# Row halves of TensorE for two heads in both attention stages of a two-layer transformer kernel

## What is computed

```python
x = x + attn_a(layernorm(x));  x = x + ffn(layernorm(x))
x = x + attn_b(layernorm(x));  x = x + ffn(layernorm(x))

# attn_a: 16 heads of 16, causal, T = 2048
att = softmax(where(causal, q @ k.T / sqrt(16), -inf))
att = att * decay_weight_matrix(T)      # zero from a lag of 511 on; the softmax sum still takes all keys
y = (att @ v) @ W_proj
# attn_b: 16 heads of 16, causal, with biases, no decay
y = layernorm(softmax(...) @ v @ Wo + bo) * gamma + beta
# ffn: gelu(x @ binarize(w1).T + b1) @ binarize(w2).T + b2
```

## Time and profile before

| | us |
|---|---|
| median of 3 runs | 2740.55 (2735.39 to 2742.51) |
| the profiled execution | 2736.11 |
| its span | 2734.4 |
| TensorE busy in the span | 2454.8 (90%) |
| VectorE busy | 1958.3 (72%) |
| ScalarE busy | 1515.6 (55%) |
| GpSimd busy | 1052.5 (38%) |

### The profile page before, as it was taken

The page is one execution under the profiler, slowest core; times in us unless marked ns, Lnnn a source line. Parts: engine busy times, 40 slices in busy tenths (PEclk is TensorE's granted clock), DMA queues, the critical chain, the costliest instruction groups (busy, mean ns, idle before and its releaser), DMA issues. The chain is left out here.

```text
span 2734.4 us, 44488 instructions
## 1 busy us (share of the span) xinstructions
PE 2454.8 (90%) x13984; PEld 1404.0 (51%) x13984; DVE 1958.3 (72%) x4863; ACT 1515.6 (55%) x3309; POOL 1052.5 (38%) x1274
## 2 busy tenths in 40 slices
PE   4959999999999999969997599999999999997788
PEld 2535545454544545437774355555555555553676
DVE  5667787777787777716663588888888888870786
ACT  1218576776767685734332056666666666664333
POOL 0037777777777777751221301000101001011653
PEclk8969999999999999989998589999999999998999
DMA  4994142332505050033544751423505234102110
GB/s 134 252 144 63 24 56 36 44 51 32 70 11 75 13 69 6 5 114 77 125 96 98 111 75 16 64 38 44 70 15 72 32 51 62 18 7 99 47 54 31
DMA packets 181847, 171.03 MB, mean 63 GB/s; under 512 B 90352, under 2 KB 131056, under 8 KB 180848
## 3 DMA queue, kind: packets, MB, share of 16 engines
q1 hardware_dynamic: 181616, 168.18, 35.0%
HBM read 105.98 MB, written 61.08 MB: 61 GB/s over the span
## 5 line engine op out<-in xcount | busy, mean ns | idle before, releaser
L704 POOL TENSOR_TENSOR att_a_wd<-att_a_wt,decay 128x256 f32<-128x256 f32 (+3 forms) x896 | 754.6, 873 | 259.8 <-PE att_a_po L907 122.7
L742 ACT ACTIVATE att_b_wt<-att_b_ps 128x512 f32<-128x512 f32 (+3 forms) x1280 | 589.4, 539 | 354.6 <-PE att_b_ps L882 352.6
L782 DVE TENSOR_REDUCE att_a_mpart<-att_a_pm 128x1 f32<-128x512 f32 x768 | 513.5, 687 | 132.2 <-PE att_a_pm L860 129.0
L782 DVE TENSOR_REDUCE att_b_mpart<-att_b_pm 128x1 f32<-128x512 f32 x768 | 503.7, 686 | 109.7 <-PE att_b_pm L860 107.7
L860 PE MATMUL att_a_pm<-att_a_kop,att_a_qop 128*128 128x512 f32 (+3 forms) x1280 | 522.6, 426 | 55.6 <-DMA att_a_qop<-att_a_qop 28.2
L742 ACT ACTIVATE att_a_wt<-att_a_ps 128x512 f32<-128x512 f32 (+3 forms) x896 | 430.8, 506 | 218.1 <-PE att_a_ps L885 131.6
L860 PE MATMUL att_b_pm<-att_b_kop,att_b_qop 128*128 128x512 f32 (+3 forms) x1280 | 503.0, 408 | 36.6 <-DMA att_b_qop<-att_b_qop 29.9
L882 PE MATMUL att_b_ps<-att_b_qop,att_b_kop 128*128 128x512 f32 (+3 forms) x1280 | 453.2, 383 | 6.6 <-ACT att_b_wt L742 3.4
L722 POOL TENSOR_SCALAR_AFFINE_SELECT att_b_wt<-att_b_wt 128x512 f32<-128x512 f32 x128 | 81.6, 637 | 867.1 <-ACT att_b_wt L742 867.1
L860 PEld LDWEIGHTS att_a_pm<-att_a_kop,att_a_qop 128*128 128x128 f32 x1280 | 240.6, 193 | 324.6 <-DVE att_a_mpart L782 130.2
L860 PEld LDWEIGHTS att_b_pm<-att_b_kop,att_b_qop 128*128 128x128 f32 x1280 | 246.3, 194 | 277.1 <-DVE att_b_mpart L782 112.0
(11 more groups left out here) (174 smaller groups left out, 2622.6 us busy)
## 6 DMA issues: line engine op xcount, KB each, us to landing
att_a_kop<-qk SPq DMA_DIRECT2D x128, 128.0 KB, 7.7
att_a_qop<-qk SPq DMA_DIRECT2D x128, 128.0 KB, 8.0
att_b_kop<-qk SPq DMA_DIRECT2D x128, 128.0 KB, 6.2
att_b_qop<-qk SPq DMA_DIRECT2D x128, 128.0 KB, 6.8
qk<-qkv_a_qk_hi SPq DMA_DIRECT2D x32, 256.0 KB, 4.7
qk<-qkv_a_qk_lo SPq DMA_DIRECT2D x32, 256.0 KB, 4.5
qk<-mid_qk_hi SPq DMA_DIRECT2D x32, 256.0 KB, 4.0
qk<-mid_qk_lo SPq DMA_DIRECT2D x32, 256.0 KB, 4.5
```

Of the source, the lines that this page charges most:

```text
L704: pool.tensor_tensor(wd[:, kq % 2, j, a:z], wt[:, kq % buffers, j, a:z], keep["decay"][:, u:u + z - a], ALU.mult).then_inc(w_decayed, 1)
L742: act.activation(wt[:, kq % buffers, j, a:CH], pe_[:, seen % EBANKS, 0:CH - a], ACT.Exp)\
L782: dve.tensor_reduce(mpart[:, c, piece, u:u + 1], pm[:, n % MBANKS, 0:w], AX.X, ALU.max, negate=True).then_inc(m_reduced, 1)
```

## The change

The 4 heads of a group become 2 pairs. Heads 0 and 1 (index j) lie on partitions 0 to 63 and heads 2 and 3 on partitions 64 to 127 of `kop` and `qop`, which are half as wide as before; there is no padding. Every M and every S of the plan now stands for two heads, a = 0 and a = 1, and issues a matmul on rows 0 to 63 and one on rows 64 to 127, into two banks. The maxima are no longer a row of `qop`: they go to a tile `mx` of their own, at row 0 and row 64, with zeros elsewhere, and each S issues a second pair of matmuls, `ones_row` x `mx`, that adds them. `mx` has one buffer for each chunk, so MC waits for the scores of the group before. The mask of att_a becomes two matmuls of 64 columns for each head. MC takes 8 transfers of half the length, the loads of a chunk take 16 of half the size, and the copy of the zero row is gone. Bank counts, buffers and widths of a unit stay.

```diff
@@ attention_plan
-            follow(number + 1, GH - 1, ("PV", c, kb))
+            follow(number + 1, 1, ("PV", c, kb))
-        for j in range(GH):
-            e.append((60.0 + CH - P * max(0, kb - TB * c), ("S", c, kb, j)))
+        for j in range(GH // 2):
+            e.append((2 * (60.0 + CH - P * max(0, kb - TB * c)), ("S", c, kb, j)))
...
-                    n += 1
+                    n += 2
@@ spaced
-            follow((3, 0.0, ("MC", c)))
+            follow((2, 0.0, ("MC", c)))
             if far(c, decayed):
-                follow((8, 0.0, ("FE", c)), (11, 0.0, ("FM", c)))
+                follow((4, 0.0, ("FE", c)), (6, 0.0, ("FM", c)))
@@ attention, tiles
-        kop = sb("kop", [P, 2, GH, T], F32R)
-        qop = sb("qop", [P, 2, NC, GH, CH], F32R)
+        kop = sb("kop", [P, 2, GH // 2, T], F32R)
+        qop = sb("qop", [P, 2, NC, GH // 2, CH], F32R)
+        mx = sb("mx", [P, NC, GH // 2, CH], F32R)
@@ SP, load
-                for r in range(PAIRS):
...
-                if g < 2:
-                    sp.wait_ge(q_padded[par], c + 1)
-                sp.dma_start(qop[MROW:MROW + 1, par, c, :, :].bitcast(F32),
-                             qop[96:97, par, c, :, :].bitcast(F32)).then_inc(qk_in[par][c], 16)
+                for a in range(2):
+                    heads = slice(head(0, a), head(0, a) + GH // 2)
+                    for r in range(PAIRS):
...
@@ SP, MC
                         sp.wait_ge(mrow_ready, done(g + d, c))
+                        if g + d > 0:
+                            sp.wait_ge(e_scores, scored(g + d - 1, c))
...
+                        for a in range(2):
+                            row = mx[HALF * a:HALF * a + 1, c, :, :].bitcast(F32)
+                            row = row.rearrange("o j (t k i) -> o (j t) k i", t=TB, k=P // SQUARE)
+                            for k in range(P // SQUARE):
+                                unit = SQUARE * k + TB * head(0, a)
+                                sp.dma_start(row[:, :, k, :], mrow[unit:unit + UNITS // 2, c, :].bitcast(F32))\
+                                  .then_inc(m_in[c], 16)
@@ TensorE, M
-                        mm = pe.matmul(pm[:, bank, 0:w], qop[:, mpar, c, j, qb * P:(qb + 1) * P],
-                                       kop[:, mpar, j, piece * CH:piece * CH + w], start=True, stop=True)
-                        mm.then_inc(m_scores, 1)
+                        for a in range(2):
+                            pe.wait_ge(m_reduced, M_UNITS * (g + d) + max(n + a + 1, MBANKS))
+                            if FARS:
+                                pe.wait_ge(f_done, FAR_UNITS * (g + d) + far_left(n + a) + MBANKS)
+                            mm = pe.matmul(pm[:, (n + a) % MBANKS, 0:w], qop[rows(a), mpar, c, j, qb * P:(qb + 1) * P],
+                                           kop[rows(a), mpar, j, piece * CH:piece * CH + w], start=True, stop=True)
+                            mm.then_inc(m_scores, 1)
@@ TensorE, S
-                        mm = pe.matmul(pe_[:, bank, 0:CH - a], kop[:, par, j, kb * P:(kb + 1) * P],
-                                       qop[:, par, c, j, a:CH], start=True, stop=not diagonal)
-                        if diagonal:
-                            mm = pe.matmul(pe_[:, bank, 0:P], keep["identr"][:, :], keep["mask_k"][:, :],
-                                           start=False, stop=True)
-                        mm.then_inc(e_scores, 1)
-                        e += 1
+                        for a in range(2):
+                            pe.wait_ge(e_weights, E_UNITS * g + max(e + a + 1, EBANKS))
+                            pe.matmul(pe_[:, banks[a], 0:CH - z], kop[rows(a), par, j, kb * P:(kb + 1) * P],
+                                      qop[rows(a), par, c, j, z:CH], start=True, stop=False)
+                        for h in range(2 if decayed and kb >= TB * c else 0):
+                            for a in range(2):
+                                pe.matmul(pe_[:, banks[a], HALF * h:HALF * (h + 1)],
+                                          keep["tri"][rows(a), (0, 1, 2, 0)[2 * a + h], :],
+                                          keep["identr"][rows(a), rows(a)], start=False, stop=False)
+                        for a in range(2):
+                            mm = pe.matmul(pe_[:, banks[a], 0:CH - z], keep["ones_row"][rows(a), :],
+                                           mx[rows(a), c, j, z:CH], start=False, stop=True)
+                            mm.then_inc(e_scores, 1)
+                        e += 2
```

144 lines of the change are left out of this document (69 added, 75 removed).

## The result

The changed kernel takes **3040.89 us** (median of 4 runs, 3039.21 to 3048.46) against 2741.53 us (2735.39 to 2746.20) for the kernel before, run beside it: 1.110 times as long, 95% interval 1.107 to 1.113. The direction was forecast, but the loss is 299 us where the sum had 47 (-24 + 67 + 4), and the time lies outside the range.

A forecast was written before the change was run, and what follows sets the result against it. TensorE was taken as the narrow bound in both attentions. From 2736.1 us, -24 (att_a) + 67 (att_b) + 4 (starts) gave 2783, and 4.4 to the median gave 2788 us, 1.7% slower; range 2665 to 2935.

The forecast's parts named there:

- -24 + 67 + 4: Whole program, in us: att_a's gain of 24, att_b's loss of 67, and 4 more for both attentions' starts.
- Overlap of a pair: TensorE, both attentions: two half-array matmuls run together, 0.26 us a pair of M (bounds 0.23 and 0.46).
- Rival 3: Both attentions: the halves do not overlap, +33 us a step in att_b, +23 in att_a, 3190 us; chance 7%.
- The chain of an att_b round: att_b, PV to PV through ScalarE and a freed score bank: 3.22 us taken, between 3.09 and 3.30, against 3.04.
- The next pair of M lies beside this: att_b round: the next maxima matmuls run alongside the wait for ScalarE, adding nothing to its 3.22 us.
- The scores gain nothing: TensorE, scores: a pair with its added maxima matmuls takes 0.49 us for two heads, against 0.46 before.
- MC's way: att_b, chunk 3: eight transfers of maxima instead of four delay the first score, +2.4 us a step; att_a nothing.
- The other 32 could gain: att_a, the 32 of 56 halves without an FX pair: could gain 9 us a step, 5 to 6 taken.
- rival 4: Both attentions: coupling is worse, FX pairs hold two maxima banks, +12 us a step att_a, +10 att_b, 2920 us; 15%.
- 24 FX pairs at 0.1 us: att_a: ScalarE bounds the halves with an FX pair, +0.1 us each, +3 in all, 2 taken a step.
- TensorE's relief of 5 to 6 us: att_a: TensorE needs 0.28 us less per half; of 9 us a step, 5 to 6 taken because VectorE limits it.
- Starts: Both attentions: 16 load issues a chunk instead of 9, +2 us each, +4 in all (bounds -2 and +8).

The follow-up runs named there:

- e5: Changed kernel with MC as four transfers, each writing both halves' rows, instead of eight: 3001.5 us.
- e1: Changed kernel's order by pairs, but with the full-array matmuls, padding, loads, maxima's row and four MC transfers of the kernel before: 2884.2 us.
- e3: Changed kernel without the ones_row matmuls, so maxima are computed and transferred but not subtracted: 2897.8 us.
- e2: Changed kernel without att_a's FX exponentials (of far maxima, on ScalarE) and the waits on them: 2921.0 us.
- e9: Kernel before without att_a's FX exponentials (of far maxima, on ScalarE): 2707.9 us.
- e15: Changed kernel with single heads, four MC transfers, no ones_row matmuls, and a full-width filler matmul before each matmul of maxima: 3019.3 us.
- e16: Kernel before with matmuls of maxima and scores both over rows 0 to 64 instead of all 128: 3345.4 us.
- e17: Kernel before with matmuls of maxima and scores both over rows 0 to 95 instead of all 128: 2785.8 us.
- e12: Changed kernel planned by single heads, with MC in four transfers and no ones_row matmuls: 2884.6 us.
- e14: Changed kernel with single heads, four MC transfers, no ones_row matmuls, and a half-width filler matmul before each matmul of maxima: 2963.6 us.
- e18: Changed kernel with single heads, four MC transfers, no ones_row matmuls, and maxima over all 128 rows, scores on halves: 3624.4 us.
- e10: Changed kernel with the plan of the kernel before, one head per item alternating between halves, one bank at a time: 2955.5 us.

## Why the prediction was wrong

**Overlap of a pair** (assumed 0.26 us, bounds 0.23 and 0.46): right, 0.23. Rival 3 is out. The weights of the `ones_row` matmul are loaded under the scores of the same half: 2095.15 to 2095.38, 0.23 us.

**The chain of an att_b round**: its links were right and its size too small. Three numbers stood there, 3.30, 3.09 and 3.22, and 3.22 was taken; the regular round is 3.34. Over 28 rounds that is 3.4 us of a step. The last step, with no maxima, shows the chain alone: rounds of 3.11 us where the earlier trace rows had 2.59. From the PV at 2763.02 to the next, the blocked score starts 2.45 on (the chain gives 0.99 + 0.34 + 0.43 + 0.60 + 0.05 = 2.41) and the PV 0.66 behind it (0.34 + 0.32 = 0.66):

```profile
2763.02 1.05 PE L928 MATMUL att_b_po<-att_b_wt,att_b_va 128*17 128x512 f32 x8
...
2765.47 0.50 PE L888 MATMUL att_b_ps<-att_b_qop,att_b_kop 64*128 64x512 f32 x1 [0.51 <-ACT att_b_wt L754]
...
2766.13 0.62 PE L928 MATMUL att_b_po<-att_b_wt,att_b_va 128*17 128x512 f32 x4
```

That step costs 15 us, where the sum had charged it 8.4 like every other.

**"The next pair of M lies beside this"** is the sentence that failed in att_b. It holds in a regular round, which is the chain's. But a pair of maxima asks for two of three banks as well, waits for VectorE, and holds up the scores behind it; with three pairs in a round it makes 4.2 us of 3.3. Forecast for rounds +6 us a step, measured +14.9 (e5's 130.1 less 115.2). The 28 wide rounds at 3.34 would be 8.4 of that; the other 6.5 are left for rounds like that with three pairs, which are in no term of the sum. By the experiments, e1 gives 7.9 to the planning and holding of banks by pairs, and 7.0 is left for the ones_row matmuls and the halves together. e3, in which taking the added matmuls away saves 11.4, says that they are more than all of that, so that the halves by themselves give some 4 us a step back (an estimate, if the savings add). "The scores gain nothing" was true of TensorE's sum, but the added matmul lies where the round's chain runs.

**MC's way**: +2.4 forecast, 4.1 measured. The stop itself is 2.2 us, as the sum had it (2.28 with eight transfers, 0.10 with four); the rest came with 7 us of half clock that went with it.

**att_a** is the largest miss, and "The other 32 could gain" is the sentence that failed there: -3 a step forecast, +15 to +19 measured. The mechanism was there as rival 4, in its own words (an FX pair holds two banks of maxima), at +12; e2 and e9 confirm it: FX costs 13 to 17 us in a step of the changed kernel and 3.8 before. The sum had 24 FX pairs at 0.1 us, cut to 2 us a step; the coupling with FX measures 10 to 13 (13 to 17 less 3.8). I gave the rival 15% and let TensorE's relief of 5 to 6 us stand against the smaller FX term. None of that relief came, not even without FX, where the step is 5.7 us longer than before. Rival 4's 2920 us is the nearest of all the cases.

**The clock** appears in no term. Every price was taken at 1.00, because the rows of before had 1.00. The changed kernel's own att_a steps give 4.0 us for 17 us of half clock, 0.23 each, so 34 us are about 8 of the 19 us that such a step lost: with 8.7 for the pairs (e1) that leaves about 2 for the rest. This split is arithmetic over three kernels and not one experiment, and at e15's price of 0.43 the clock alone would be 15 of the 19 us. That rows in use bring the clock down is shown in the kernel before (e16, e17); that this is what happens on the row halves too is inferred: half clock is 0 to 11 us an att_a step with full-array pairs (e1), 17 to 34 with pairs of halves, and 48 to 82 with single heads on halves and no ones (e12). The closest two are e1 and e3, which both have pairs and no added matmuls: 0 to 11 us on full arrays, 24 to 47 on halves. But halves also shorten TensorE's work, and these two can't tell fewer rows from less work. e14, e15 and e18, meant to close this, did not. What share of the changed kernel's half clock comes from its rows and what from its stops stays open.

**Starts**: +4 us forecast, -2.5 found. From the first load to the first mark att_a takes 1.0 us less than before and att_b 1.5, although a chunk has 16 loads now; the padding and the copied zero row, for which the first maximum waited, are gone. What failed is the rest of the start, which the sum put at nothing: up to the first mark of chunk 3 att_a takes 11 us more (134.0 instead of 122.7) and att_b 10 (126.9 instead of 116.7).

No kernel with row halves beat the kernel before. By e16 and e17 that kernel owes its clock to padding that looked like waste.

## What to carry to other kernels

A unit of work that is doubled to feed an engine also doubles what it holds: count the banks that it takes, and every reader that must be done before the next one starts, before counting the engine's cycles. On TensorE a matmul with zeros in the unused rows cost no time here (115.2 us a step with 65 rows or with 128) and can be worth having; take rows out only after looking at what the granted clock does. And where a chain's bounds are 3.09 and 3.30, a second stream through the same queue is a reason to go to the upper end or past it.

## What the runs showed of the hardware

- Two 64-row fp32r matmuls of 512 columns on different halves run wholly side by side: 0.23 us for both. When they are not planned as a pair they start 0.01 us apart too (e10, 2121.85 and 2121.86).
- The granted clock of TensorE depends on how many rows its matmuls use, with all else equal: 2745 us at 128 rows, 2786 at 96, 3345 at 65, with TensorE busy 99% of a step that was at half clock for most of its length. It fell behind a wait of 0.82 us; with 128 rows the same wait left it up.
- A matmul over 65 rows takes what one over 128 takes while the clock is full: step 115.20 us in both.
- A change between 64-row and 128-row matmuls costs 0.20 us each time at full clock (0.43 instead of 0.23), and between 64 and 65 rows at half clock 0.3 us (0.72 instead of 0.43).
- In one program, steps with the same instructions settle into different forms, 135.1 or 148.0 us, according to the clock that they find.
